# Moving the routing dot products on VectorE and the layer norm on ScalarE within each step of a fused SSM and routed-attention kernel

## The reference

```
x = x + ssm(layernorm(x))                       # causal convolution along the sequence
x = x + ffn(layernorm(x))
# ffn(x):
light = light_attn(x)      # layernorm again, qkv, 8 heads of 64, windows of 64 that see
                           # the window before, their own and the one behind, softmax, w_out
s = einsum('bnd,rd->brn', x, routing_token)     # one dot product of 512 for each token, for
                                                # q and for kv
scores = coor_descent(s)   # 50 iterations; the top 512 (q) and 1024 (kv) tokens are taken
out = light + (heavy_attn of the chosen tokens, scattered, the others get null_q)
```

## Time and profile before

| What | Value |
|---|---|
| median of 3 runs | 4843.7 us (4834.42, 4843.70, 4843.73) |
| the profiled execution: time, span | 4843.73 us, 4842.0 us |
| PE busy | 4309.7 us (89%) |
| DVE busy | 2927.1 us (60%) |
| ACT busy | 2040.4 us (42%) |
| POOL busy | 858.7 us (18%) |
| mean granted PE clock | 0.937 |

### The profile page before, as it was taken

How to read it: one execution, slowest core, us unless ns; L and a number is a source line. 1 busy time by engine, 2 the same in 40 slices (tenths; PEclk the granted TensorE clock), 3 DMA queues, 4 the chain that set the end, 5 groups by cost and what they waited for, 6 DMA issues and landing times. The chain is left out here.

```text
span 4842.0 us, 96011 instructions
## 1 busy us (share of the span) xinstructions
PE 4309.7 (89%) x37058; PEld 3586.5 (74%) x37058; DVE 2927.1 (60%) x5381; ACT 2040.4 (42%) x5308; POOL 858.7 (18%) x678
## 2 busy tenths in 40 slices
PE   6687756999999999999999997438999999999999
PEld 6576645888888888888888886426777777777776
DVE  5687745666665666666666645784644645646545
ACT  4443313444444444444444433313443434434434
POOL 0122200222222222222222223101101101011011
PEclk9998968999999999999999998558999999999999
DMA  6868851222212221222222112002202112012010
GB/s 220 232 156 208 212 145 38 62 62 66 63 57 67 60 63 60 64 64 64 61 64 65 56 47 83 0 0 53 42 14 49 19 38 52 8 47 45 14 40 12
DMA packets 322760, 335.89 MB, mean 69 GB/s; under 512 B 20848, under 2 KB 218736, under 8 KB 322288
## 3 DMA queue, kind: packets, MB, share of 16 engines
q1 hardware_dynamic: 243952, 262.35, 18.8%
q0 software_dynamic: 12288, 33.56, 3.3%
q10 hardware_dynamic: 66048, 33.56, 2.6%
HBM read 203.04 MB, written 76.02 MB: 58 GB/s over the span
## 5 line engine op out<-in xcount | busy, mean ns | idle before, releaser
L1209 POOL TENSOR_TENSOR l_prob<-l_prob,l_inv 128x768 f32<-128x768 f32 x256 | 370.2, 1467 | 1817.4 <-DVE l_inv L1185 1817.4
L1000 ACT ACTIVATE l_prob<-l_ps_s,l_neg_max 128x192 f32<-128x192 f32 (+2 forms) x1152 | 463.5, 428 | 1.7 <-DVE l_neg_max L1161 0.5
L2062 DVE TENSOR_REDUCE h_neg_max<-h_ps_s 128x1 f32<-128x1024 f32 x256 | 313.3, 1224 | 201.3 <-PE h_ps_s L1849 199.2
L1983 ACT ACTIVATE h_prob<-h_ps_s,h_neg_max 128x1024 f32<-128x1024 f32 x256 | 285.7, 1116 | 341.8 <-DVE h_neg_max L2065 310.7
L1161 DVE TENSOR_REDUCE l_neg_max<-l_ps_s 128x4 f32<-128x768 f32 (+2 forms) x288 | 256.7, 924 | 250.6 <-PE l_ps_s L867 249.7
L1861 PE MATMUL h_ps_t<-ident,h_prob 128*128 128x128 f32 x2048 | 277.4, 279 | 7.6 <-ACT h_prob L1983 7.6
L1873 PE MATMUL h_ps_o<-h_probs_t,h_val 128*64 128x128 f32 x4096 | 278.4, 279 | 0.0
L1873 PEld LDWEIGHTS h_ps_o<-h_probs_t,h_val 128*64 128x64 f32 x4096 | 218.6, 137 | 80.0 <-issue 55.0
L988 ACT ACTIVATE l_k_t<-l_ps_a,w_bias_k 128x512 f32<-128x512 f32 x64 | 44.0, 687 | 532.8 <-PE l_ps_s L867 280.9
L1861 PEld LDWEIGHTS h_ps_t<-ident,h_prob 128*128 128x128 f32 x2048 | 222.8, 141 | 60.4 <-issue 42.9
L1000 ACT ACTIVATION_READ_ACCUMULATOR l_prob<-l_ps_s,l_neg_max 128x1 f32 (+1 forms) x1152 | 254.7, 221 | 0.0
(11 more groups left out here) (383 smaller groups left out, 11490.1 us busy)
## 6 DMA issues: line engine op xcount, KB each, us to landing
xin<-in_L_attn_x_dram SPq DMA_DIRECT2D x32, 1024.0 KB, 5.3
xg<-in_L_attn_x_dram SPq DMA_DIRECT2D x64, 512.0 KB, 10.3
toep_back<-taps_padded ACTq DMA_DIRECT2D x32, 1024.0 KB, 11.3
x<-xg SPq DMA_DIRECT2D x64, 512.0 KB, 9.7
l_xin<-x SPq DMA_DIRECT2D x128, 256.0 KB, 3.2
l_xres<-x SPq DMA_DIRECT2D x128, 256.0 KB, 3.3
l_val_side<-l_val SPq DMA_DIRECT2D x256, 128.0 KB, 3.2
out_dram<-l_res SPq DMA_DIRECT2D x128, 256.0 KB, 2.0
```

The source lines that it names most:

```text
L1000: last = nc.scalar.activation(prob[t % 2][rows, h, pair, cols], ps_s[rows, h, pair, cols], ACT.Exp, bias=neg_max[rows, t % 2, h, pair:pair ...
L1209: nc.gpsimd.tensor_tensor(mine, mine, spread(inv[:, t % 2, h, :], [1, PAIRS], [0, WIN + P]), ALU.mult).then_inc(p_normed, 1)
L1983: nc.scalar.activation(prob[i % 2][:, :].rearrange("p (a k) -> p a k", a=2), ps_s[i % 2][:, :, :], ACT.Exp, bias=neg_max[:, qt % 2, h:h + ...
L2062: nc.vector.tensor_reduce(at, ps_s[i % 2][:, :, :].rearrange("p a k -> p (a k)"), AX_X, ALU.max, negate=True).then_inc(max_step, 1)
```

## The change

Three moves, all in `light_phase`; nothing is added or left out.

1. On ACT, `layernorms(g + 1)` moves from behind the copy of PE's second unit to the very start of the step.
2. On DVE, the dot products of tile g leave the middle of step g (behind the residual, ahead of the maxima). Those of tile g+1 stand at the end of step g, right behind `keep_xt_lo` and ahead of `tile_stats` and `squares`.
3. The dot products of tile 0 stand ahead of the first step.

```diff
                 def body(g, j, live):                      # ACT
+                    if live(-1):
+                        layernorms(g + 1, (j + 1) % NCH, (g - j) + GT * ((j + 1) // GT + 1))
                     if live(3):
                         wait(act, u2_made, g - 2)
                         if live(7) and (j + 1) % GT in (0, 3):
                             wait(act, s_made, g - 6)
                         keep_unit(ps_a, units(j)[1], u2_kept)
-                    if live(-1):
-                        layernorms(g + 1, (j + 1) % NCH, (g - j) + GT * ((j + 1) // GT + 1))
                     if live(9):
                         wait(act, o_made, g - 8)
...
                 keep_xt_lo(0, 0)                           # DVE, ahead of the steps
+                routing_dots(0, 0)
...
                         nc.vector.tensor_tensor(res[:, j % 2, :], ps_c[:, :], xres[:, j % 2, :], ALU.add).then_inc(res_made, 1)
-                    if live(0):
-                        routing_dots(g, j)
                     if live(7):
                         t = (j - 7) % NCH
                         wait(v, s_made, g - 6)
...
                     if live(-1):
                         keep_xt_lo(g + 1, j + 1)
+                        routing_dots(g + 1, (j + 1) % NCH)
                     if live(-7):
                         tile_stats(g + 7, (j + 7) % NCH, (g - j) * 2 + 16 * ((j + 7) // AHEAD + 1))
                         if j % GT == 0:
                             squares(g + 4, (j + 4) % NCH, chain_at(g, j, 4))
```

## The result

The changed kernel is slower: 4869.5 us median (4865.3 to 4872.1, 4 runs) against 4842.2 us of the kernel before (4834.4 to 4843.7, 4 runs), a ratio of 1.0058 with a 95% interval of 1.0041 to 1.0077. Forecast was 4842.0 us, and "same". The time lies above the forecast's range.

A forecast was written before the change was run, and what follows sets the result against it. The prediction took PE to bound the kernel, so only PE's waits could be won. Terms -1.2 - 0.4 - 1.4 + 1.45 = -1.6 us against the profiled 4843.73 us gave 4842 us, range 4833 to 4852.

The forecast's parts named there:

- PE bounds the phase, and moves pay only in what PE waits for: Light phase: it goes at PE's pace; DVE or ACT moves gain at most PE's steady waits, 17.7 us.
- The dot products meet POOL and hold still: DVE behind `keep_xt_lo`: two-SBUF-input instructions stand still while POOL runs one; dot products cost 3.4 us, not 1.4.
- The long chain: DVE's chain of statistics every fourth step: L1089 starts 1.45 us later, at about 1313.1 instead of 1311.68.
- The next thing for which PE waits is the copy of the first unit, needed only before the scores. Cost 0: DVE in steps without the chain: it ends its step 3.4 us later and idles less before the residual; cost 0.
- ACT every fourth step, cost 0: ACT's table load, roots, norms and second-unit copy come later, but at_hi starts when it did; cost 0.
- The thin cover: ACT every fourth step: slack of 0.1 us on ACT and 0.35 us behind it, expected to hold.
- the slower rival: ACT about 28 times: L1089 about 2.5 us late makes PE wait for at_lo; about 4855 us, chance 0.10.
- Steps 6 and 7 of a sequence, 0.17 us each: ACT: at_hi starts 0.17 us earlier without norms ahead, shortening PE's 0.7 us wait; gain 7 x 0.17 = 1.2 us.
- The first steps: Start of the phase: norm waits shrink 0.4 us, the 5.2 us wait gains 1.4, step 9 loses 1.45.
- The clock: PE behind the 5.2 us wait: if a 3.8 us wait leaves the granted clock up, 2.5 us more are won.
- Rival 1: POOL isn't interrupted between queued instructions, so L1089 starts 2.5 us late; 10 to 17 us slower, about 4855, chance 0.10.

The follow-up runs named there:

- The experiment with one input: Changed kernel with the two dot products replaced by maxima over x2n alone, so the router gets other numbers; 4830.6 us, ratio 0.9977.
- the experiment with POOL behind: Changed kernel, but POOL begins its multiplications only when both dot products of the step are done; 4841.0 us, ratio 0.9993.
- the dot products alone: Dot products at their new place on DVE, ACT's list as in the kernel before; 4872.8 us, ratio 1.0056 against the kernel before.
- the third experiment: Changed kernel with PE's waits for the scores' inputs moved three quarters into the second unit; 4834.1 us, ratio 0.9980 against the kernel before.

## Why the prediction was wrong

- **PE bounds the phase, and moves pay only in what PE waits for: right.** The 27.3 us of the phase are those of the medians.
- **The dot products meet POOL and hold still: right in kind and nearly in size.** Forecast was 3.4 us for both, measured 3.2 (1488.77 to 1491.93), in nearly every step. The experiment with one input, the row of L1046 and the experiment with POOL behind show that it is the second SBUF input and POOL. The long chain ended 1.1 us later in its step (L1089 6.6 us behind the step's start before, 7.7 after), forecast 1.45.
- **"The next thing for which PE waits is the copy of the first unit, needed only before the scores. Cost 0": this step failed.** DVE is late by nearly what was worked out, but PE asks for the copy ahead of the second unit, 5.6 us into the step, and not ahead of the scores at 8.5. Measured price: 0.5, 1.15, 0.5 and 1.5 us in steps 3, 7, 11 and 15, about 3.6 a sequence and 29 in eight sequences, of which some 1.5 are won back elsewhere. With the wait 2.1 us further down the list it is nothing.
- **The small copy (L1126) was not counted.** It moved with the dot products and is held by POOL too: 8 to 10 us of the loss. It costs that only because PE asks at 5.6 us, as above.
- **ACT every fourth step, cost 0: right.** at_hi starts 12.1 us into the step before and after, and PE waits for at_lo in no more steps. The thin cover, from which the slower rival took its place, held; ACT's idle time before at_hi went from 1.14 to 0.78 us.

```profile
1321.14 1.28 ACT L982 ACT_TABLE_LOAD   x1 [7.07 <-DVE l_square L1089]
...
1325.32 0.60 ACT L1016 ACTIVATE l_at_hi<-l_ps_d 128x512 fp32r<-128x512 f32 x1 [0.78 <-PE l_ps_d L896]
```

- **Steps 6 and 7 of a sequence, 0.17 us each: right.** The wait of 0.72 us is 0.59.
- **The first steps: right to some tenths.** 5.2 us became 3.8; step 9 lost 1.03 us, forecast 1.45; the wait for the norms shrank by 0.5, forecast 0.4. In step 9 the dot products alone lose the 1.03 us and the one-input instructions nothing, which points to DVE's lateness, as forecast. The clock did not stay up: the first matmul behind the shorter wait still took 0.80 us, against 0.47 for the one behind the wait at 799.27 below.
- **Rival 1** was right in sign and in that a thin cover of DVE's lateness breaks, but had another place, and its mechanism (POOL never interrupted) is refuted: the first dot product (1488.77 to 1490.05) ends 1.3 us before POOL's two multiplications do (1491.38).

The trace before held the row that would have caught it. In step 7 of the phase PE stands still ahead of its second unit until DVE's copy of the first has ended, 0.85 us behind that unit:

```profile
798.41 0.75 DVE L1053 TENSOR_SCALAR l_q_t<-l_ps_b,w_bias_q 128x512 f32<-128x512 f32 x1 [0.85 <-PE l_ps_b L673]
```

```profile
799.27 0.47 PE L671 MATMUL l_ps_a<-l_xt_hi,w_qkv_hi 128*128 128x512 f32 x1 [0.89 <-issue]
```

It was there once and put down to "issue". The start of the second unit, 799.27, is 0.11 us behind the end of that copy, 799.16. That row gives the place of the wait: ahead of the second unit. In this early step there is no output product yet; in the steady steps it lies ahead of the second unit too, and the due time follows from the steady rows before the change, here the first and the second unit of a step 15:

```profile
1477.63 0.48 PE L671 MATMUL l_ps_b<-l_xt_hi,w_qkv_hi 128*128 128x512 f32 x1
...
1483.24 0.40 PE L671 MATMUL l_ps_a<-l_xt_hi,w_qkv_hi 128*128 128x512 f32 x1
```

They are 5.61 us apart. The copy of the first unit ended 3.8 us into the step then, 1.8 us ahead of the second unit, and DVE had idled 0.85 us before it. The two together are 2.7 us of cover, less than the 3.4 us of two held dot products.

What stays open: the third experiment gains 9.7 us by the medians and 5.3 us by the phases of one profiled execution, and why PE's clock comes back earlier in some executions than in others was not tried. What lies outside the phase, and the edits don't touch, moved by up to 12 us from one profiled execution to the next.

## What to carry to other kernels

When a step is made later, look up each wait for it in the list of the engine that waits, and take as its due time the place of the wait, not the place of the instruction that needs the data: on an in-order engine everything behind the wait is late. When an instruction of VectorE with two SBUF inputs, or a plain copy within SBUF, moves, ask what GpSimd does at the new place, and count the small instructions that move with it. If such a move is wanted, either let GpSimd start behind it or put the consumer's wait further down; each brought the time back to that of before here, the first but for 0.27 us in step 15.

## What the runs showed of the hardware

The hold-up goes both ways and by turns. The first dot product waits for POOL's first multiplication, runs, POOL's second runs while DVE waits again, and POOL's multiplication that stood behind a dot product took up to 1.92 us, not 1.47. All instructions of POOL's line 1209, after and before (least/median/most ns):

```profile
L1209 POOL TENSOR_TENSOR l_prob<-l_prob,l_inv x256: 1467/1470/1919, 814.7 to 2999.1; 128x768 f32<-128x768 f32 x128
```

```profile
L1209 POOL TENSOR_TENSOR l_prob<-l_prob,l_inv x256: 1464/1467/1471, 814.1 to 2970.1; 128x768 f32<-128x768 f32 x128
```

The forecast did not have the small copy, one input of 32 elements a partition, held as well (0.18 us became 1.06, and 1.46 with POOL behind the dot products), while a reduction with one input of 512 wasn't (683 ns). The Trainium skill has both in "SBUF — State Buffer", Who interferes with whom: copies can enter a mode with two ports and contend, a reduction on trn2 never does. The rows agree.
